# Cross-attention scores of a perceiver block: from one 128x128 product per four heads to sixteen 32x32 array tiles

## The reference, cut to what matters

```python
# per batch element: query (32, 512), context (257, 512), H = 16 heads of D = 32
q = (query @ Wq).reshape(B, L, H, D).transpose(0, 2, 1, 3)
k = (key @ Wk).reshape(B, S, H, D).transpose(0, 2, 1, 3)
v = (value @ Wv).reshape(B, S, H, D).transpose(0, 2, 1, 3)
attn = softmax(einsum('bhld,bhsd->bhls', q * SCALE, k))     # (B, 16, 32, 257)
x = einsum('bhls,bhsd->bhld', attn, v).transpose(0, 2, 1, 3).reshape(B, L, C)
return x @ Wo + bo
```

## Time and profile before

| | |
|---|---|
| median of three runs | 2831.87 us (2829.82 to 2831.88) |
| the profiled execution | 2830.43 us |
| span of the profiled execution | 2828.5 us |
| mean granted clock of TensorE | 0.986 of full speed |
| busy, share of the span | PE 96%, weight loads 58%, DVE 59%, ACT 44%, POOL 28% |
| scores of cross-attention | 1536 products, from 157 to 1933 us |

### The profile page before, as it was taken

One profiled execution on the slowest core, in us unless ns is written; L12 is line 12 of the kernel. 1 busy time (PEld: TensorE's weight loads), 2 busy tenths in 40 slices (PEclk: granted clock), 3 DMA queues, 4 the chain that ended last, 5 costly groups with the idle time before them and its releaser, 6 DMA issues. The chain is left out here.

```text
span 2828.5 us, 53617 instructions
## 1 busy us (share of the span) xinstructions
PE 2710.3 (96%) x17866; PEld 1630.2 (58%) x17866; DVE 1657.7 (59%) x3650; ACT 1241.4 (44%) x2899; POOL 778.0 (28%) x1530
## 2 busy tenths in 40 slices
PE   7999999999999999999999999996889989998999
PEld 4555555555555555555555555554556656666666
DVE  7645555555555555555555555554676776676675
ACT  4444444444444444444444444442334434444444
POOL 2133333333333333333333333331121121111110
PEclk9999999999999999999999999998999999999999
DMA  4312111211111111111111111102000000000000
GB/s 139 107 44 70 55 53 53 65 53 53 56 62 53 53 59 58 46 42 42 42 42 42 42 47 44 42 20 87 8 31 16 16 30 15 15 30 15 15 23 16
DMA packets 72687, 126.98 MB, mean 45 GB/s; under 512 B 12336, under 2 KB 36912, under 8 KB 71856
## 3 DMA queue, kind: packets, MB, share of 16 engines
q1 hardware_dynamic: 72624, 126.15, 13.9%
HBM read 113.26 MB, written 12.85 MB: 45 GB/s over the span
## 5 line engine op out<-in xcount | busy, mean ns | idle before, releaser
L824 DVE SCALAR_TENSOR_TENSOR kT_lo<-psum,kT_hi 128x512 f16<-128x512 f32 x256 | 175.4, 691 | 432.1 <-ACT kT_hi L740 432.1
L744 ACT ACTIVATE v_hi<-psum 128x512 f16<-128x512 f32 x256 | 152.8, 597 | 550.3 <-PE psum L935 550.3
L129 POOL TENSOR_TENSOR c_lo<-ctx_raw,c_hi 128x1024 f16<-128x1024 f32 x128 | 272.5, 2129 | 430.7 <-ACT c_hi L736 404.7
L935 PE MATMUL psum<-c_hi,xWk_hi 128*128 128x512 f16 x1024 | 388.1, 379 | 0.5 <-PEq L149 0.5
L935 PE MATMUL psum<-xWv_hi,c_hi 128*128 128x512 f16 x1024 | 388.1, 379 | 0.0
L935 PE MATMUL psum<-xWv_lo,c_hi 128*128 128x512 f16 x1024 | 388.1, 379 | 0.0
L935 PE MATMUL psum<-xWv_hi,c_lo 128*128 128x512 f16 x1024 | 388.1, 379 | 0.0
L935 PE MATMUL psum<-c_hi,xWk_lo 128*128 128x512 f16 x1024 | 388.1, 379 | 0.0
L935 PE MATMUL psum<-c_lo,xWk_hi 128*128 128x512 f16 x1024 | 388.1, 379 | 0.0
L830 DVE SCALAR_TENSOR_TENSOR v_lo<-psum,v_hi 128x512 f16<-128x512 f32 x256 | 177.0, 691 | 357.4 <-ACT v_hi L744 357.4
L750 ACT ACTIVATE e<-psum,neg_max 128x257 f32<-128x257 f32 x512 | 236.2, 474 | 298.1 <-DVE neg_max L819 298.1
(11 more groups left out here) (222 smaller groups left out, 5700.9 us busy)
## 6 DMA issues: line engine op xcount, KB each, us to landing
ctx_raw<-in_ctx_main SPq DMA_DIRECT2D x128, 512.0 KB, 3.4
xs<-in_x SPq DMA_DIRECT2D x8, 1024.0 KB, 5.5
v_rep<-v_last_rows SPq DMA_DIRECT2D x512, 16.0 KB, 2.4
late_raw<-in_w_t SPq DMA_DIRECT2D x16, 512.0 KB, 3.9
xb<-in_x SPq DMA_DIRECT2D x16, 512.0 KB, 3.7
out<-res_out SPq DMA_DIRECT2D x32, 256.0 KB, 2.1
sign_dram<-signs_out SPq DMA_DIRECT2D x16, 256.0 KB, 2.5
sign<-sign_dram SPq DMA_DIRECT2D x4, 1024.0 KB, 8.6
```

Of the source, the lines that this page charges most:

```text
L129: nc.gpsimd.tensor_tensor(c_lo[u // 2][:, :, u % 2, :], c_raw[u % 2][:, :, :], c_hi[u // 2][:, :, u % 2, :], ALU.subtract).then_inc(c_lo_d ...
L744: nc.scalar.mul(v_hi[u][:, t, :], v_bank(t), W_UNSCALE).then_inc(v_hi_done, 1)
L824: nc.vector.scalar_tensor_tensor(out=kT_lo[r][:, m, :, 0:S], in0=k_bank(m), scalar=W_UNSCALE, in1=kT_hi[r][:, m, :, 0:S], op0=ALU.mult, op ...
L935: mm = nc.tensor.matmul(bank, a, b, start=(n == 0), stop=(n == len(steps) - 1))
```

## The change

The scores are computed per head. A head needs 32 features x 32 tokens as weights, which is one 32x32 tile of the array: its row is set by the partitions of the query and key features (h), its column by the partitions of the result (g). The 16 heads of an element thus fill the 16 tiles. There are now 3 passes x 16 heads = 48 products of 32x32 weights with 257 columns, with the pass outermost and the row of the tile changing fastest. The head (g, h) now lands on partitions 32g of bank h, where it was on partitions 32h of bank g. Everything that depends on that layout moves with it: the last value row is stored in its natural order, `outputs` takes the value columns of the four heads h of all chunks (a strided moving operand), and the rows of the output weight are loaded in another order, by four DMAs in place of one.

The queries are no longer spread. GpSimd copies the 128 x 4 x 32 queries of an element as they are, in two copies, into one of two buffers, and may do so one element earlier. The waits of `score` stand ahead of the last product of the second value half, and no longer between that product and the scores.

```diff
-                nc.scalar.mul(vl[:, :].rearrange("p (h g d) -> p g h d", h=4, g=KC),
-                              v_last_bank.rearrange("p (g h d) -> p g h d", h=4, g=KC),
-                              W_UNSCALE).then_inc(vl_done, 1)
+                nc.scalar.mul(vl[:, :], v_last_bank, W_UNSCALE).then_inc(vl_done, 1)
...
+            def load_output_weight():
+                rows = late_w[0].rearrange("(i d) (g n) -> g d i n", i=HPG, g=KC)
+                to = late_raw.rearrange("p o (c n) -> p (o c) n", c=KC)
+                for g in range(KC):
+                    sp.dma_start(to[32 * g:32 * g + 32, :, :], rows[g]).then_inc(late_landed, 16)
...
-            def spread(b, contexts):
-                past(pool, s_ps, b)
+            def stage_queries(b, u, contexts):
+                past(pool, s_ps, b - 1)
                 past(pool, c_lo_done, contexts)
...
-                for h in range(HPG):
-                    rows = slice(32 * h, 32 * h + 32)
-                    nc.gpsimd.tensor_copy(bd_hi[rows, :, h, :],
-                                          heads_hi[rows, :, bass.ds(b * L, L)]).then_inc(bd_ready, 1)
-                    nc.gpsimd.tensor_copy(bd_lo[rows, :, h, :],
-                                          heads_lo[rows, :, bass.ds(b * L, L)]).then_inc(bd_ready, 1)
+                for heads, q in ((heads_hi, q_hi), (heads_lo, q_lo)):
+                    nc.gpsimd.tensor_copy(q[u % 2][:, :, :], heads[:, :, bass.ds(b * L, L)]
+                                          ).then_inc(q_ready, 1)
...
-            def values(b, u, t):
+            def values(b, u, t, score_next=None):
                 past(pe, v_lo_done, ST * (b - 1) + t + 1)
...
+                for n, (a, b) in enumerate(steps):
+                    if score_next and n == len(steps) - 1:
+                        score_may_start(*score_next)
+                    mm = nc.tensor.matmul(v_bank(t), a, b, start=(n == 0), stop=(n == len(steps) - 1))
+                mm.then_inc(v_ps, 1)
...
-                for g in range(KC):
-                    mm = run(psum[:, g, 0:S + 1],
-                             [(q[:, g, :, :].rearrange("p h l -> p (h l)"), k[u // 2][:, g, u % 2, 0:S + 1])
-                              for q, k in passes(bd_hi, bd_lo, kT_hi, kT_lo)])
+            def score(i, u):
+                steps = passes(q_hi[u % 2], q_lo[u % 2], kT_hi, kT_lo)
+                for n, (q, k) in enumerate(steps):
+                    for g in range(KC):
+                        for h in range(HPG):
+                            rows = slice(32 * h, 32 * h + 32)
+                            mm = nc.tensor.matmul(psum[32 * g:32 * g + 32, h, 0:S + 1], q[rows, g, :],
+                                                  k[u // 2][rows, g, u % 2, 0:S + 1], start=(n == 0),
+                                                  stop=(n == len(steps) - 1))
                 mm.then_inc(s_ps, 1)
...
-                for g in range(KC):
-                    cols = slice(g * P, (g + 1) * P)
-                    mm = run(out_bank[:, g, :], [(p[:, t, cols], v[:, t, cols]) for t in range(ST)
-                                                 for p, v in passes(pT_hi, pT_lo, v_hi[u % 2], v_lo[u % 2])])
+                for h in range(HPG):
+                    cols = slice(h * P, (h + 1) * P)
+                    mm = run(out_bank[:, h, :].rearrange("p (g d) -> p g d", g=KC),
+                             [(p[:, t, cols], v.rearrange("p t (g h d) -> p t h g d", g=KC, h=HPG)[:, t, h])
+                              for t in range(ST)
+                              for p, v in passes(pT_hi, pT_lo, v_hi[u % 2], v_lo[u % 2])])
```

More of the change, by code:

```diff
@@ L539, in cross_attention @@
         v_lo = [sb_in(ctx, f"v_lo{u}", [P, ST, D], F16) for u in range(2)]
-        bd_hi = sb_in(ctx, "bd_hi", [P, KC, HPG, L], F16)
-        bd_lo = sb_in(ctx, "bd_lo", [P, KC, HPG, L], F16)
+        q_hi = [sb_in(ctx, f"q_hi{u}", [P, KC, L], F16) for u in range(2)]
+        q_lo = [sb_in(ctx, f"q_lo{u}", [P, KC, L], F16) for u in range(2)]
         signs_out = sb_in(ctx, "signs_out", [P, 2 * D], F16)
@@ L571, in cross_attention @@
         late_lo_done = sem_in(ctx, "late_lo_done")
-        names = ["bd_clear", "bd_ready", "k_col", "last_done", "k_ps", "v_ps",
+        names = ["q_ready", "k_col", "last_done", "k_ps", "v_ps",
                  "s_ps", "p_ps", "pv_ps", "k_hi_done", "k_lo_done", "v_hi_done", "v_lo_done", "max_done",
@@ L575, in cross_attention @@
                  "o_norm_done", "o_T_done", "o_hi_done", "o_lo_done"]
-        (bd_clear, bd_ready, k_col, last_done, k_ps, v_ps, s_ps, p_ps, pv_ps,
+        (q_ready, k_col, last_done, k_ps, v_ps, s_ps, p_ps, pv_ps,
          k_hi_done, k_lo_done, v_hi_done, v_lo_done, max_done, neg_done, e_done, pT_hi_done, pT_lo_done,
@@ L659, in _ @@
                 load_last(b, b)
-            with sp.Fori(0, LATE) as i:
+            load_output_weight()
+            quad(0)
+            with sp.Fori(1, LATE) as i:
                 quad(i, late=True)
@@ L675, in _ @@
         def _(pool):
-            nc.gpsimd.memset(bd_hi[:, :, :, :], 0.0).then_inc(bd_clear, 1)
-            nc.gpsimd.memset(bd_lo[:, :, :, :], 0.0).then_inc(bd_clear, 1)
-            pool.wait_ge(bd_clear, 2)
-            def spread(b, contexts):
-                past(pool, s_ps, b)
+            def stage_queries(b, u, contexts):
+                past(pool, s_ps, b - 1)
                 past(pool, c_lo_done, contexts)
@@ L702, in last_token @@
                 b = i * 4 + u
-                pool.wait_ge(bd_ready, 2 * HPG * (b + 2 if more else b + 1))
+                pool.wait_ge(q_ready, 2 * (b + 2 if more else b + 1))
                 pool.wait_ge(e_done, KC * (b + 1))
@@ L714, in step @@
                 if more:
-                    spread(b + 1, b + 4 if ahead else BATCH)
+                    stage_queries(b + 1, u + 1, b + 4 if ahead else BATCH)
                 last_token(i, u, more)
@@ L720, in step @@
                     low_context(nc, pool, contexts, b + 4, u)
-            spread(0, 0)
-            pool.wait_ge(bd_ready, 2 * HPG)
+            stage_queries(0, 0, 0)
+            pool.wait_ge(q_ready, 2)
             last_keys(0, 0)
@@ L762, in high_late @@
             def high_late(n, c):
-                act.wait_ge(late_landed, 16 * (n + 1))
+                act.wait_ge(late_landed, 16 * (n + KC))
                 nc.scalar.mul(late_hi_w[:, bass.ds(n * 2, 1), c * D:(c + 1) * D],
@@ L943, in keys, with score_may_start @@
                                 for w, c in passes(wk_hi, wk_lo, c_hi[r], c_lo[r])]).then_inc(k_ps, 1)
-            def values(b, u, t):
+            def values(b, u, t, score_next=None):
                 past(pe, v_lo_done, ST * (b - 1) + t + 1)
                 rows = slice(t * P, (t + 1) * P)
[L948 to L952, removed]
+                steps = [(c[:, k, u % 2, rows], w[:, k, :]) for k in range(KC)
+                         for c, w in passes(c_hi[u // 2], c_lo[u // 2], wv_hi, wv_lo)]
+                for n, (a, b) in enumerate(steps):
[3 more added lines that the diff above has]
+                mm.then_inc(v_ps, 1)
+            def score_may_start(i, u):
                 b = i * 4 + u
-                pe.wait_ge(bd_ready, 2 * HPG * (b + 1))
+                pe.wait_ge(q_ready, 2 * (b + 1))
                 pe.wait_ge(k_col, 2 * (i * 2 + u // 2 + 1))
@@ L994, in step @@
                 if more:
-                    values(b + 1, (u + 1) % 4, 1)
+                    values(b + 1, (u + 1) % 4, 1, score_next=(i, u + 1) if u < 3 else (i + 1, 0))
             for m in range(KC):
@@ L999, in _ @@
             values(0, 0, 0)
-            values(0, 0, 1)
+            values(0, 0, 1, score_next=(0, 0))
             def sum_units(j):
```

## The result

The changed kernel takes 2769.53 us (median of four, 2767.97 to 2770.90) against 2831.13 us in the same comparison: ratio 0.9783, 95% interval 0.9766 to 0.9800. It is faster by 61.6 us; the forecast was 2783, a gain of 49, with 2740 to 2858 as range. The profiled span went from 2828.5 to 2766.2 us, 62.3 less. From the last element's scores to the end of the program the profiled executions of all kernels here take 895.3 to 902.1 us, the longer ones mostly at a lower mean clock, so where two medians lie closer than that the elements' distances decide.

What follows compares the result with a forecast made beforehand. TensorE's instruction stream was taken as the bound. Scores of 0.634 us for tiles plus 0.245 for borders replace 1.32, saving 0.44 us in 111 elements, 49 us: 2831.87 - 49 = 2783 us, range 2740 to 2858.

Steps and rivals of the forecast that it cites:

- What bounds: Cross-attention: TensorE's instruction stream sets the stage's end, busy 99.32 of 100 us, unless another engine is late.
- Who gets the gain: Cross-attention: 111 elements gain 0.44 us each; 16 behind feed-forward weights and the last but one gain nothing.
- The sum: Whole kernel: 49 us off a median of 2831.87 us gives 2783 us.
- the 0.65 us of slack: First two quads, eight elements: TensorE could reach the transposes 0.65 us earlier without waiting for the exponentials.
- the tiles: Scores: 48 pairs of weight load and product at 0.0132 us each, 0.634 us an element.
- The geometric mean: Scores: 0.0132 us a pair, taken between the near bounds of 0.0069 and 0.0253 us.
- The borders: Array shape changes around each element's scores: 0.245 us, the whole pipeline depth of 0.163 going in, half coming out.
- the forecast case: Scores: pairs between 0.009 and 0.018 us, total 2765 to 2813 us, middle 2783; chance 0.38.
- the pair as bound: Rival in the scores: every pair costs 0.0253 us, scores 1.214 us without shape changes, total 2847 us; chance 0.22.
- rows of the array one behind the other: Rival in the scores: tiles of one row run serially, +36 us, 2868; chance 0.09, including no overlap at all.
- the strided operand: The 24 output products reading 4 runs of 32 values: at worst 1.25 us an element, 160 in all; taken as nothing.
- Full streaming: Rival in the scores: all sixteen tiles stream at once, three passes take 0.33 to 0.39 us, total 2725 to 2765; chance 0.27.

Runs made afterwards that it cites:

- e8: The kernel before with only the waits of the scores moved ahead of the last value product, scores still 12 products of 128x128: 2832.14 us, ratio 0.9999.
- e12: The changed kernel with GpSimd's two query copies again behind the scores of the element before: 2766.95 us, ratio 0.9767.
- e7: The changed kernel with the magnitudes of a weight piece on DVE moved from ahead of the third element's maximum to behind it: 2750.18 us, ratio 0.9711.
- e10: The kernel before with the magnitudes of a weight piece moved behind the third element's maximum: 2822.08 us, ratio 0.9960.
- e3: The changed kernel with the tile's column changing fastest and its row slowest: 2766.38 us, ratio 0.9771.
- e6: The changed kernel with one more pass of 16 tiles ahead of the last value product, so four shape changes an element, not two: 2818.32 us, ratio 0.9944.
- e4: The changed kernel with the three passes of one tile one behind the other: 2813.38 us, ratio 0.9932.

## Why the prediction was right, and where its sizes were off

- *What bounds:* right. TensorE's stream sets the stage before and after, and of the other parts the waits and copies measured nothing (e8, e12).
- *Who gets the gain:* right. The exponentials kept their distance from the value products, the transposes in ordinary elements never waited, and the 16 elements behind a piece of weights gained under 0.05 us each. e7 and e10 show the swallowed part at 10 us, where 16 x 0.44 = 7 was left out by the forecast.
- *The sum:* 111 x 0.44 = 49 was forecast. The distances between scores give the 62.3 by which the span fell: 109 ordinary elements 62.7, the 16 together 0.6, the ninth element 0.24, and the last distance -1.25. The ninth element waits (13.65 us) because its maximum stands behind the last late weights and, besides, behind the clearing of a buffer, which the 0.65 us of slack from one row had missed:

```profile
267.22 0.48 DVE L918 MEMSET mag_sum<- 128x512 f32 x1
```

The last distance took 13.79 us against 12.54, and it is the clock. Windows before and after, around the output products of the last element but one:

```profile
1927.00:1931.00 4.00, 3.88 (x36) 2.59 (x37) 1.90 (x8) 0.00 (x0) 0.00 (x0) 1.00 0.00 0
1865.00:1869.00 4.00, 4.00 (x29) 2.80 (x28) 1.75 (x6) 0.00 (x0) 0.00 (x0) 0.77 0.01 4
```

The granted clock was 0.77 where it had been 1.00, so part of the window was at 1.2 and not 2.4 GHz, and output products start 0.107 us apart in place of 0.056. TensorE had waited 1.59 and 1.57 us just ahead, 1.01 and 1.56 before. But e3 and e12 have the same two waits, a clock of 1.00 there and 12.54 us: the loss came and went between executions and is not shown to belong to the change.
- *The term that was mis-sized, the tiles:* 0.634 us from 13.2 ns a pair. They take 0.54: 0.43 to the start of the last tile and 0.107 to stream it. The geometric mean stood for ignorance of the mechanism, and the price is no single number: 3.3 ns for a queued pair, 8.3 ns for one behind the queue, and a late start of the third pass between. Both bounds held. The low one, 6.9 ns, was approached by the first two passes: 32 pairs in 0.28 us with their streaming, 8.7 ns each.
- *The borders:* 0.245 was forecast, 0.093 going in and 0.209 - 0.107 = 0.102 coming out measured, 0.195. e6 gives 0.21 for a second pair of them. So a border is neither free nor the whole depth of the pipeline, 0.163, and the forecast's reason for taking one as twice the other (0.163 and 0.082) did not hold. The rule of the Trainium skill that a change of mode drains the engine ("TensorEngine Tiling (Array Packing)", Key Properties) fits in that there is a cost.
- *The bounds of the forecast case:* by its own terms, pairs between 0.009 and 0.018 us and 0.245 of borders in 111 elements give 2761 to 2808, where 2765 to 2813 was written. Nothing hangs on it: the measured time is inside both.
- *The rivals:* the pair as bound at 25.3 ns is refuted by the starts at 3.3 ns; rows of the array one behind the other by the 16 starts within 0.05 us and by e3; the strided operand by the output products, which still record 220 ns and start 0.056 us apart. Full streaming, 2725 to 2765, came closer than its chance of 0.27 let expect: 2769.53 lies between it and the middle of the forecast. The Trainium skill's rule of one product and 4 ns for each further tile ("TensorE: Matmul & The Clock Gate", Part 3) holds here for the first 32 pairs, at 3.3 ns. That 2765, worked out from it, came within 5 us is luck: it had 0.39 us for the tiles, which took 0.54, and 0.33 for the borders, which took 0.195.

## What to carry to other kernels

Where a block-diagonal operand only serves to fill the array, independent tiles are worth it: 48 tiles of 32x32 did in 0.73 us, borders included, what 12 full products did in 1.32. Keep tile products in groups of some 32 pairs, as far as these runs go, put products that share a tile as far apart as there are tiles, and cross between tile shapes rarely, at about 0.1 us each way. When a bounding engine gets faster, look for the places where it waits already: they give nothing until the work in front of the wait is moved, and moving it is then worth twice what it was (19 us here against 10 before, or 17.1 against 8.3 by the elements alone).

## What the runs showed of the hardware that was not expected

- The edge at some 32 pairs: within a pass tiles start 3.3 ns apart up to the 32nd pair, and the 33rd starts 0.31 us behind the first tile, whether the second pass streams 257 columns or 64; from there the pace is 8.3 ns. With the pass innermost (e4) the 34th pair's weights load as late as in the changed kernel, 0.31 us behind the first tile. A queue would explain it; none was shown.
- TensorE starts products out of program order across tiles. With three products of a tile in a row it started eleven tiles' first products, 10 ns apart, before any second one (e4). The twelfth tile's three products, past the edge, start one behind the other, 0.11 us apart.
- The order of rows and columns of the array within a pass makes no difference (13.32 us an element either way).
- The two borders cost much the same, 0.09 and 0.10 us, though products on 128 rows end at one and products on 32 rows at the other.
